# Casting weights in the DMA and deferring work in a fused attention and expert layer on eight cores

## What is computed

```python
x = x + _layernorm(attn(_layernorm(x), w_qkv, w_out))       # 16 heads of 128, causal
x = x + _layernorm(ffn(_layernorm(x), weight, lora_A, lora_B, router_w))
# attn: softmax(q k^T / sqrt(128)) v, then @ w_out
# ffn:  x @ weight^T + 2 * sum over the top 2 of 8 experts of w_e * (x @ A_e^T) @ B_e
```

## Time and profile before

| quantity | us |
|---|---|
| median of 2 runs | 3221.38 (3214.53 to 3228.22) |
| the profiled execution | 3227.05 |
| its span on the slowest core (core 3) | 3225.5 |
| spans of the eight cores | 3205.0 to 3225.5 |

### The profile page before, as it was taken

One profiled execution on the slowest core, in us unless ns is written; L12 is line 12 of the kernel. 1 busy time (PEld: TensorE's weight loads), 2 busy tenths in 40 slices (PEclk: granted clock), 3 DMA queues, 4 the chain that ended last, 5 costly groups with the idle time before them and its releaser, 6 DMA issues.

```text
span 3225.5 us, 29462 instructions; the slowest of 8 cores (3205.0 to 3225.5 us)
## 1 busy us (share of the span) xinstructions
PE 1992.4 (62%) x9552; PEld 916.1 (28%) x9552; DVE 875.4 (27%) x2483; ACT 652.2 (20%) x1394; POOL 126.1 (4%) x292
## 2 busy tenths in 40 slices
PE   1228777786787778677768877069904353453543
PEld 0113333333333333333333333034402121221221
DVE  4441111111111111111111111135533434434334
ACT  1112233124313322432332233000000000000000
POOL 0000000000000000000000000000000000000000
PEclk9998867786776778677768766589956676766766
DMA  2131110111011011101101100422260000000000
GB/s 77 68 104 40 40 40 1 40 40 35 5 40 40 1 40 40 29 12 40 40 1 40 40 1 1 156 96 75 79 229 33 26 14 26 14 27 27 14 27 26
DMA packets 47571, 138.34 MB, mean 43 GB/s; under 512 B 3648, under 2 KB 36544, under 8 KB 37056
## 3 DMA queue, kind: packets, MB, share of 16 engines
q1 hardware_dynamic: 42816, 102.90, 9.9%
q0 software_dynamic: 4608, 33.56, 2.8%
HBM read 119.67 MB, written 16.78 MB: 42 GB/s over the span
## 4 chain that ended last, share of the span: by engine, by line
PE 54%; DVE 20%; issue 11%; ACT 8%; DMA 5%; DVEq 1%; ACTq 0%; SPq 0%; POOL 0%; POOLq 0%
PE P_qkv L295 22%; PE P_qkv L387 8%; PE P_b L643 7%; ACT expT L359 4%; DVE sst L150 4%; PE P_e L481 3%; PE P_o L481 3%; DVE att L400 3%; DMA wo_st<-w_out 2%; PE P_sc L351 2%; PE P_t L409 2%; DVE wbf L277 2%; DMA wst<-weightT 2%; DVE sst L396 1%; PE P_qkv L351 1%
## 5 line engine op out<-in xcount | busy, mean ns | idle before, releaser
L295 PE MATMUL P_qkv<-A,wbf 128*128 128x512 bf16 x3072 | 714.5, 398 | 47.1 <-DVE wbf L277 47.1
L295 PEld LDWEIGHTS P_qkv<-A,wbf 128*128 128x128 bf16 x3072 | 311.3, 102 | 445.4 <-issue 145.2
L603 PE MATMUL P_u<-cbuf,xln 128*128 128x128 bf16 x256 | 52.3, 268 | 440.2 <-ACT xln L593 402.2
L387 PE MATMUL P_qkv<-Vaug,expT 128*128 128x129 bf16 x2176 | 254.7, 291 | 38.9 <-ACT expT L359 37.8
L643 PE MATMUL P_b<-A,x2T 128*128 128x512 bf16 x1024 | 273.2, 412 | 0.0
L396 DVE RECIPROCAL sst<-P_qkv 128x1 f32<-128x1 f32 x256 | 43.0, 168 | 834.0 <-PE P_qkv L387 834.0
L387 PEld LDWEIGHTS P_qkv<-Vaug,expT 128*128 128x128 bf16 x2176 | 198.9, 131 | 87.6 <-issue 70.9
L409 PE MATMUL P_t<-cbuf,att 128*128 128x128 bf16 x256 | 66.4, 259 | 242.9 <-DVE att L400 242.9
L359 ACT ACTIVATE expT<-P_sc,cbuf 128x512 bf16<-128x512 f32 x320 | 206.2, 712 | 20.4 <-PE P_sc L351 15.2
L359 ACT ACTIVATE expT<-P_qkv,cbuf 128x512 bf16<-128x512 f32 x320 | 208.0, 726 | 0.0
L188 ACT ACTIVATE sst<-sst,cbuf 128x1 f32<-128x1 f32 x64 | 18.8, 294 | 832.6 <-DVE sst L184 832.6
(11 more groups left out here) (69 smaller groups left out, 1426.8 us busy)
## 6 DMA issues: line engine op xcount, KB each, us to landing
wstage<-wqkv SPq DMA_DIRECT2D x16, 3072.0 KB, 14.2
expT<-x SPq DMA_DIRECT2D x16, 1024.0 KB, 6.0
wo_st<-w_out SPq DMA_DIRECT2D x16, 1024.0 KB, 4.9
wo_st<-x POOLq DMA_DIRECT2D x16, 1024.0 KB, 5.1
wst<-weightT SPq DMA_DIRECT2D x16, 1024.0 KB, 5.9
out<-ost POOLq DMA_DIRECT2D x16, 1024.0 KB, 4.2
wst<-bflat SPq DMA_DIRECT2D x1, 1024.0 KB, 4.7
cbuf<-consts SPq DMA_DIRECT2D x1, 68.0 KB, 2.2
```

The source lines that it names most:

```text
L295: e.matmul(P_qkv[:, _q:_q + 512], wbf[:, 384 * _c + 128 * _m: 384 * _c + 128 * _m + 128], A1[:, 2048 * _c + _q: 2048 * _c + _q + 512], sta ...
L387: _q=qt: e.matmul(P_qkv[:, _a:_a + 129], expT[:, 512 * _i + 128 * _u: 512 * _i + 128 * _u + 128], Vaug[:, 129 * _i:129 * _i + 129], start= ...
L603: e.transpose(_pt[:, 0:128], xln2[:, 2048 * _p + 128 * _c: 2048 * _p + 128 * _c + 128], sid),
```

## The change

Six things are done together.

- Weights are loaded by GpSimd's queue straight to bf16, the DMA casting on its way: a head's `wqkv` into one of two halves of `wbf`, `w_out` in two loads of 8 MB (of source), `weightT` in two, and the router's weights, `at` and `bflat` in one each. The staging buffers and VectorE's casts go. The factor 2 of `bflat` moves to `sw8`.
- The transpose of `att` for tile qt is emitted after the PV matmuls of tile qt+1 (`pend_T`, `drain_T`), with two halves of `att` and two reciprocals.
- The mask multiply goes from GpSimd to VectorE.
- In stage 3, ScalarE normalises PSUM into `ntmp` and VectorE adds x.
- In stage 4, ScalarE copies the transposes, scales the `su` slices, takes two of the four copies from `P_b` and forms `x2s`.
- In stage 4, all 32 narrow matmuls come first and the 64 wide ones behind them, so the router's chain starts before the wide ones.

```diff
-                wrdy = B.emit("sync", lambda s, _h=h: s.dma_start(
-                    out=wstage[:].rearrange("p (c f) -> p c f", f=384),
-                    in_=wqkv[_h].rearrange("(c p) f -> p c f", p=128)),
-                    waits=B.gw(["wstage"]), inc=c["ld_w"], inck=16)
-                wbf_rdy = B.emit("vector",
-                                 lambda e: e.tensor_copy(wbf[:], wstage[:]),
-                                 waits=[(c["ld_w"], wrdy)] + B.gw(["wbf"]),
-                                 inc=c["dve"])
-                B.sg(["wstage"], c["dve"], wbf_rdy)
+                wpar = h % 2
+                wsem = c["ld_w0"] if wpar == 0 else c["ld_w1"]
+                wrdy = B.emit("gpsimd", lambda s, _h=h, _p=wpar: s.dma_start(
+                    out=wbf[:, 6144 * _p:6144 * _p + 6144]
+                    .rearrange("p (x f) -> p x f", f=384),
+                    in_=wqkv[_h].rearrange("(x p) f -> p x f", p=128)),
+                    waits=B.gw([("wbf", wpar)]), inc=wsem, inck=16)
...
-                B.sg(["wbf"], c["pe"], c["pe"].v)
+                B.sg([("wbf", wpar)], c["pe"], c["pe"].v)
...
+                    def drain_T(item):
+                        _h, _qt, _p, _attv = item
+                        pt2 = P_t1 if _qt % 2 == 0 else P_t2
+                        pbank2 = 6 + _qt % 2
+                        tv2 = B.emit("tensor", lambda e, _pt=pt2, _pp=_p:
+                                     e.transpose(_pt[:, 0:128],
+                                                 att[:, 128 * _pp:
+                                                     128 * _pp + 128], sid),
+                                     waits=[(c["dve"], _attv)]
+                                     + B.gw([pbank2]), inc=c["pe"])
+                        B.sg([("att", _p)], c["pe"], tv2)
...
-                            pv = B.emit("gpsimd", lambda e, _i=i, _o=s_off:
+                            pv = B.emit("vector", lambda e, _i=i, _o=s_off:
...
+                        pend_T.append((h, qt, apar, attv))
+                        if len(pend_T) > 1:
+                            drain_T(pend_T.pop(0))
+            while pend_T:
+                drain_T(pend_T.pop(0))
...
+            for hh in range(2):
+                B.emit("gpsimd", lambda s, _h=hh: s.dma_start(
+                    out=wo_bf[:, 16384 * _h:16384 * _h + 16384]
+                    .rearrange("p (x f) -> p x f", f=2048),
+                    in_=w_out[1024 * _h:1024 * _h + 1024, :]
+                    .rearrange("(x p) f -> p x f", p=128)),
+                    waits=(scope_w if hh == 0 else []),
...
-                dv = B.emit("vector", lambda e, _c=chk, _s=stg: e.tensor_copy(
-                    wo_bf[:, 2048 * _c:2048 * _c + 2048],
-                    wo_st[:, _s:_s + 2048]),
-                    waits=[(c["ld_wo"], lv)], inc=c["dve"])
-                B.sg([("wo_st", 0)], c["dve"], dv)
-            wo_all = c["dve"].v
+            wo_all = c["ld_wo"].v
...
+                nv = B.emit("scalar", lambda e, _P=P, _r=rstd, _m=negmr:
+                            e.activation(ntmp[:], _P[:], AF.Identity,
+                                         bias=_m, scale=_r),
+                            waits=[(c["dve"], dve_ln)] + B.gw(["ntmp"]),
+                            inc=c["act"])
+                x2v = B.emit("vector", lambda e, _t=t: e.tensor_tensor(
+                    A1[:, 2048 * _t:2048 * _t + 2048], ntmp[:], xio2[:],
+                    ALU.add),
+                    waits=[(c["act"], nv), (c["ldg"], xrdy)], inc=c["dve"])
...
+            scope2 = [(c["pe"], outproj_pe), (c["dve"], outproj_dve),
+                      (c["act"], outproj_act)]
+            for hh in range(2):
+                B.emit("gpsimd", lambda s, _h=hh: s.dma_start(
+                    out=A2[:, 16384 * _h:16384 * _h + 16384]
+                    .rearrange("p (x f) -> p x f", f=2048),
+                    in_=weightT[1024 * _h:1024 * _h + 1024, :]
+                    .rearrange("(x p) f -> p x f", p=128)),
+                    waits=(scope2 if hh == 0 else []),
...
+            B.emit("gpsimd", lambda s: s.dma_start(
...
+                out=sbf[:], in_=bflat_in), inc=c["ld_wt"], inck=16)
+            wT_all = c["ld_wt"].v
...
-                    dv = B.emit("vector", lambda e, _p=par, _c=ch, _pt=pt:
-                                e.tensor_copy(
+                    av = B.emit("scalar", lambda e, _p=par, _c=ch, _pt=pt:
+                                e.activation(
                                     x2T[:, 2048 * _p + 128 * _c:
                                         2048 * _p + 128 * _c + 128],
-                                    _pt[:, 0:128]),
-                                waits=[(c["pe"], tv)], inc=c["dve"])
-                    B.sg([bank], c["dve"], dv)
+                                    _pt[:, 0:128], AF.Copy),
+                                waits=[(c["pe"], tv)], inc=c["act"])
+                    B.sg([bank], c["act"], av)
...
-                        wts = gw_all + [
-                            (c["dve"], max(x2T_rdy, wT_dve, small_dve)),
-                            (c["act"], small_act)]
+                        wts = gw_aux + [(c["act"], x2T_act),
+                                        (c["ld_wt"], wT_all)]
...
+                aux_done = c["pe"].v
+                gw_base = B.gw([0, 1, 2, 3])
+                for ch in range(NCH):
                     for f in range(4):
...
+                    uav = B.emit("scalar", lambda e, _a=aux0, _x=ex:
+                                 e.activation(
+                                     su[:, 16 * _x:16 * _x + 16],
+                                     P_x[:, _a + 8 + 16 * _x:
+                                         _a + 8 + 16 * _x + 16],
+                                     AF.Identity, scale=sw8[:, _x:_x + 1]),
...
+                    eng = "vector" if f < 2 else "scalar"
...
+                xsv = B.emit("scalar", lambda e, _t=t, _m=negmr3:
+                             e.activation(x2s[:],
+                                          A1[:, 2048 * _t:2048 * _t + 2048],
+                                          AF.Identity, bias=_m, scale=1.0),
```

More of the change, by code:

```diff
@@ L150, in plan_ln @@
                         e.bn_stats(sst[:, _b + 6 * _j: _b + 6 * _j + 6], _f(_j))),
-                       waits=(list(pre_waits) + B.gw([("sst", par)])) if j == 0 else (),
+                       waits=(list(pre_waits) + B.gw([("sst", par), ("rcp", par)])) if j == 0 else (),
                        inc=(c["dve"] if j == 3 else None))
@@ L395, in build_program @@
                         avv = c["pe"].v
[L396 to L404 removed]
+                        apar = qt % 2
@@ new lines, in build_program @@
+                        fv = B.emit("vector", lambda e, _a=avsl, _p=apar:
+                                    e.reciprocal(
+                                        stc(_p, 36),
+                                        P_qkv[:, _a + 128:_a + 129]),
+                                    waits=[(c["pe"], avv)]
+                                    + B.gw([("rcp", apar)]), inc=c["dve"])
+                        attv = B.emit("vector", lambda e, _a=avsl, _p=apar:
+                                      e.tensor_scalar(
+                                          att[:, 128 * _p:128 * _p + 128],
+                                          P_qkv[:, _a:_a + 128],
+                                          stc(_p, 36), None, ALU.mult),
+                                      waits=[(c["dve"], fv)]
+                                      + B.gw([("att", apar)]),
@@ L405, in build_program @@
                                       inc=c["dve"])
+                        B.sg([("rcp", apar)], c["dve"], attv)
                         B.sg([bank], c["dve"], attv)
-                        pt = P_t1 if qt % 2 == 0 else P_t2
-                        pbank = 6 + qt % 2
-                        tv = B.emit("tensor", lambda e, _pt=pt: e.transpose(
-                            _pt[:, 0:128], att[:], sid),
-                            waits=[(c["dve"], attv)] + B.gw([pbank]),
-                            inc=c["pe"])
@@ L647, in build_program @@
                                             2048 * _c + 512 * _f + 512],
[L648 to L653 removed]
+                                        start=(_c == 0), stop=False),
+                               waits=(gw_base if (ch == 0 and f == 0) else ()))
                 fv = B.emit("vector", lambda e, _a=aux0: e.max(
```

221 lines of the change are left out of this document (68 added, 153 removed).

## The result

The changed kernel takes 2745.42 us (median) against 3230.0 for the kernel before, timed on the same chip: a ratio of 0.8507 [0.8485, 0.8529]. The forecast of 2800 was 55 us too high; the range of 2715 to 2925 holds the result. The profiled execution of the changed kernel took 2744.29 us.

The account below looks back on a forecast made before the run. No engine bounds the kernel throughout; work is handed from one to the next. From the profiled 3227.05 us, -253 - 85 - 37 - 11 - 40 + 6 = -420 gives 2807, forecast as a 2800 median, range 2715 to 2925.

Parts of the forecast that it names:

- The heads: Attention heads: deferred transposes hide most waits for att, and the weights' cast goes; 15.8 us a head, 253 us saved.
- The clock: Heads: without pauses full clock holds from block 3's scores into the projections; 5.3 us a head, 85 us saved.
- The loads: Big weight loads become casting DMAs: 37 us saved ahead of the output projection, 11 saved before the expert matmuls.
- at 271 it takes 62: Load of w_out: 16.8 MB at 271 GB/s, plus 2 us for landing, 64 us in place of 100.7.
- The far side (a slow cast): Load of w_out: if casting halves the rate of 222 GB/s, it takes 151 us, 50 lost.
- The expert tiles: Expert stage: router's chain hidden under wide matmuls, copies shared with ScalarE; net 2.5 us a tile, 40 us for 16.
- 32 at 0.11 are 3.5 us at half clock ... 1.7 lost: Expert tiles: narrow matmuls standing alone no longer hide their weight loads under wide ones; 1.7 us lost a tile.
- The clock doesn't hold: Heads: the clock still falls at each block's end, so the 85 us don't come; 2885 us, chance 0.20.
- VectorE becomes the bound: Heads' blocks: masks, reciprocals and scalings share one queue; half of the 253 comes, clock stays down; 3010 us, chance 0.10.
- Fast loads and clock: Wide loads stream at 347 GB/s and the clock also holds in blocks 1 and 2; 2746 us, chance 0.15.
- The transposes still wait: Heads: VectorE's chain stays longer than the PV group, so transposes wait for att; about 3085 us, chance 0.04.
- slower by the cast: The two big loads: casting DMAs so slow that other gains are lost; 3375 us at 50 GB/s, chance 0.03.

Follow-up runs that it names:

- the plain-load run: The changed kernel with the first 8.4 MB of w_out loaded once more, uncast, ahead of the two casting loads: 2772.18 us, 0.862 to the kernel before.
- the pipelined kernel: The changed kernel with the next expert tile's layer norm and transposes issued beside this tile's wide matmuls: 2450.55 us, 0.7618 to the kernel before.
- the run with staged weights: The changed kernel with the heads' weights loaded in float32 by SyncE and cast by VectorE again, one buffer each: 2826.1 us, 0.8787 to the kernel before.

## Why the prediction was right, and where it was off

**The heads** were forecast at 111.2 - 15.8 - 5.3 = 90.1 us and take 88.8. The steps laid out tile by tile held: blocks of 5.7, 9.3, 10.5 and 14.0 us in the second head, against 5.8, 8.9, 10.7 and 14.2 forecast (11.9 less the clock's 1.2, 16.2 with the gap, less 2.0). The usual head has 5.4, 8.4, 10.9 and 15.0, which is the same sum. The waits sit where they were put, at the first transposes behind the masks, and 53.7 us against "about 60". Taking the deferral back and adding it alone both confirm the size.

The 15 us that the heads gained beyond the forecast (353 for 338) are not a step of it. They stand in the execution that it started from, on the core that its rows show. The projections of core 3's seventh and eighth head, from the chain before (start, us):

```profile
902.79 50.60 PE P_qkv L295 x192
1021.37 51.87 PE P_qkv L295 x192
```

The first of these stretches on cores 0 and 3 (columns as above), and the group of all heads' projections on core 3, then on core 0:

```profile
902.80:953.40 50.60, 46.13 (x204) 20.35 (x204) 7.08 (x9) 4.74 (x15) 0.00 (x0) 0.94 0.21 62
902.80:953.40 50.60, 50.58 (x192) 20.78 (x192) 4.84 (x7) 2.39 (x4) 0.00 (x0) 0.81 0.22 62
```

```profile
L295 PE MATMUL P_qkv<-A,wbf 128*128 128x512 bf16 x3072 | 714.5, 398 | 47.1 <-DVE wbf L277 47.1
```

```profile
L295 PE MATMUL P_qkv<-A,wbf 128*128 128x512 bf16 x3072 | 701.5, 393 | 47.1 <-DVE wbf L277 47.1
```

The two took 50.6 and 51.9 us, where the core's other heads take 43 to 44, and the granted clock in the first was 0.81 where core 0 had 0.94. Core 2 shares this, the other six cores do not; what lowered the clock there, no run shows. Over all heads the projections took 714.5 us on core 3 and 701.5 on core 0. From first projection to last transpose the heads took 1774.6 us on core 3 and 1756 to 1760 on cores 0 and 4 to 7. After, all eight cores have 1420 to 1423. A core without such heads thus gained about 337 us, and 253 + 85 = 338 were forecast. That the two agree to a microsecond is luck, as block 3's clock shows.

**The clock** was the forecast's second guess. In the projections it is right in kind and size: "half of those 4.1 us, 2.1" a head. Before, a head's projections take 701.5 / 16 = 43.8 us, after 668.4 / 16 = 41.8, and the first 4 us are at 1.00 in every head. In the blocks it is right in part: in thirteen of sixteen heads block 3 does not keep the full level, and it takes 15.0 us for 14.2. Block 1 made that good (8.4 us at 0.75, for 8.9 at the clock it had before).

**The loads.** The step "at 271 it takes 62" was mis-sized. The rate read from a loop that stops for casts is that loop's, and dividing by its DMA share (347 GB/s), as the rival did, overshot: the two casting loads ran at 315. That makes 8 us at w_out and 10 at the expert load, of which the forecast had the direction and the two sides. The far side (a slow cast) is excluded by these loads themselves and by the plain one beside them. All eight cores load at that time in every trace here, so how fast one would load alone is not shown.

An interference of VectorE with GpSimd's writing of descriptors, which the Trainium skill's "SBUF — State Buffer" (Who interferes with whom) describes, costs nothing that TensorE waits for: the weights land in 15.5 us (page of the changed kernel: `wbf<-wqkv`, 1536.0 KB at the destination) against 14.2, and no wait on them is left. No run here isolates it. And the loads of w_out stay under the 358 GB/s of the Trainium skill's "DMA: Bandwidth & Descriptors" (Specifications): 315, from the windows of the plain-load run.

**The expert tiles** gained 3.9 us each and not 2.5. The step that was mis-sized is "32 at 0.11 are 3.5 us at half clock ... 1.7 lost". They are through in 2.5 us, wait for the first wide one included. From the first narrow matmul to `su` a tile is 3.1 us shorter in the mean (20.3 to 17.1), where the forecast had 3.8 - 1.7 = 2.1; so some 0.6 was lost and not 1.7. Putting them back among the wide ones costs 4.1. The small terms read from the third tile are near their forecasts: the copies from `P_b` saved 1.1 (1.2), `x2s` cost 0.7 (0.8), and ScalarE's copies of the transposes cost 0.35 (nothing): from the start of `xln` to the first narrow matmul 8.7 us for 8.3. Some 0.5 a tile is not placed, and no run takes the moves to ScalarE back one by one. Over 16 tiles the term was 22 us too small.

**The rivals.** "The clock doesn't hold" fell with the 1.00 at the start of the projections in all sixteen heads. "VectorE becomes the bound" had a true part, the masks in front of the reciprocals, worth 46 us as their reordering showed, and not 212. "Fast loads and clock" (2746) is nearest in time, but by luck: it wants 25 us from a clock that holds in blocks 1 and 2, and block 1 has 0.68 in the second head and at most 0.76 in the others, while 22 us came from the tiles and 15 from the two slow heads before. "The transposes still wait" and "slower by the cast" are excluded by the wait list and by the plain load.

One sign of being wrong came true to the letter: TensorE waits for VectorE's masks, 24.9 us in 65 times (`PE P_qkv L407 <- DVE expT L389`). Before, the same matmuls waited 37.8 us for the exponentials, so the sign was too strict and nothing was lost by it. None of the other signs of being wrong came. The prediction also gives "slower" two chances, 0.03 among the rivals and 0.02 in the summary; nothing hangs on the difference.

The gap of 63 us between the forecast's 2807 for the profiled execution and 2744 is thus, within 1 us: the two slow heads of core 3 before 15, loads 18, tiles 22, the first stage 6 (5 forecast for a delay that did not come), the output projection 1.

## What to carry to other kernels

In queues that run strictly in order, an instruction that is emitted one step too early holds up everything behind it: look for a wait that recurs once a loop pass, and emit its consumer one pass later before thinking about faster operations. Price such a pause with what it does to the clock behind it. Before a difference of a few us per pass is explained, read the same group on other cores and look at its count: the page shows the slowest core, which is where a disturbance sits (714.5 us for 701.5), and a count below the program's (3008 for 3072) makes busy time look smaller than it is. When a load moves to another engine's queue, list what computes there: here masks on GpSimd cost 124 us with the load behind them and gained some 12 to 20 with the load ahead. And after each gain read the wait list again: the largest row left (323.6 us) was worth as much (295 us) as the change's best edit.

## What the runs showed of the hardware that was not expected

- Narrow matmuls (8 and 128 columns) run in pairs of about 0.13 us when they stand together: in the timeline of the pipelined kernel 16 pairs take from 2045.61 to 2047.7, at a granted clock of 0.50, the 1.2 GHz level.
- A DMA that casts f32 to bf16 read at 315 GB/s on each of eight cores at once, where one that doesn't cast ran at 286, alone in flight.
- The granted clock stayed at the 2.4 GHz level through block 3 of the second head, with TensorE busy for 9.51 of 14.00 us, but it was 0.77 in the fifteenth head's, with 11.87 of 15.01. It was 1.00 at the start of the projections of all sixteen heads, and 0.57 there behind a pause of 3.8 us.
- The slowest core need not be slow for its program: cores 2 and 3 before ran two heads' projections at 0.79 to 0.81 of full clock while the other six did not, and so did cores 2 and 3 in the run with staged weights.
